# Last stage of a gated cross-attention block: row statistics of ten batches moved from VectorE to ScalarE and GpSimd

## The reference

```python
def _layernorm(x, axis=-1, eps=1e-05):
    m = jnp.mean(x, axis=axis, keepdims=True)
    v = jnp.var(x, axis=axis, keepdims=True)
    return (x - m) / jnp.sqrt(v + eps)

x = x + jnp.tanh(g_xattn[0]) * _L0_xattn_ref(_layernorm(x), ctx, ctx)
x = x + jnp.tanh(g_ffn[0]) * _L0_ffn_ref(_layernorm(x), w_gate, w_up, w_down)
x = x + jnp.tanh(g_xattn[1]) * _L1_xattn_ref(_layernorm(x), ctx, ctx, 16)
# last block: block_quant has blocks of 32 along the columns
h = einsum('bsk,nk->bsn', block_quant(_layernorm(x)), block_quant(w_fc)) + b_fc
h = jax.nn.gelu(h, approximate=False)
y = einsum('bsk,nk->bsn', block_quant(h), block_quant(w_proj)) + b_proj
x = x + jnp.tanh(g_ffn[1]) * y
```

## Time and profile before

| | |
|---|---|
| Times of three runs | 814.9, 815.8, 817.67 us; median 815.8 |
| The profiled execution | 816.15 us, of which the traced span is 814.0 us |
| Busy over the span | PE 701.7 us (86%), DVE 691.9 (85%), ACT 486.2 (60%), POOL 431.4 (53%) |
| Costliest groups of the last stage | `f_hup` on POOL 58.2 us, `f_ht` on ACT 32.4, `f_h` (gelu) on ACT 34.9 |
| Granted TensorE clock, mean of the span | 0.941 of full speed |

### The profile page before, as it was taken

The page is one execution under the profiler, slowest core; times in us unless marked ns, Lnnn a source line. Parts: engine busy times, 40 slices in busy tenths (PEclk is TensorE's granted clock), DMA queues, the critical chain, the costliest instruction groups (busy, mean ns, idle before and its releaser), DMA issues.

```text
span 814.0 us, 16554 instructions
## 1 busy us (share of the span) xinstructions
PE 701.7 (86%) x5075; PEld 516.7 (63%) x5090; DVE 691.9 (85%) x1230; ACT 486.2 (60%) x955; POOL 431.4 (53%) x331
## 2 busy tenths in 40 slices
PE   1476999999999998789999999999999876877685
PEld 1365888888888876556666666666666433544454
DVE  5996888888888878779999999989898649999995
ACT  3354555455454443348887787888788674566653
POOL 3634664656656555644445555554444526665553
PEclk9588999999999999889999999999999687999998
DMA  8800000000000000010000000000001000100011
GB/s 271 252 33 0 2 1 1 0 0 0 0 0 1 1 2 0 1 53 2 3 3 1 1 1 2 1 1 1 1 1 53 2 1 0 40 26 26 27 39 52
DMA packets 17719, 18.35 MB, mean 23 GB/s; under 512 B 1670, under 2 KB 16912, under 8 KB 17680
## 3 DMA queue, kind: packets, MB, share of 16 engines
q1 hardware_dynamic: 17084, 17.66, 6.6%
q10 hardware_dynamic: 596, 0.20, 0.1%
HBM read 13.39 MB, written 4.19 MB: 22 GB/s over the span
## 4 chain that ended last, share of the span: by engine, by line
PE 56%; DVE 22%; issue 9%; ACT 6%; POOL 3%; DMA 1%; DVEq 1%; POOLq 0%; ACTq 0%
PE ps_o L547 9%; PE a_ps_t L586 7%; PE a_ps_pv L642 7%; PE a_ps_s L627 5%; PE a_ps_m L606 5%; DVE f_ps_small L1643 4%; PE ps_gu L511 4%; PE ps_gu L513 4%; PE ps_gu L512 4%; DVE f_hcode L1659 4%; PE a_ps_t L606 3%; DVE maxima L1558 2%; PE a_ps_pv L650 2%; ACT stack_t L953 1%; ACT probs L962 1%
## 5 line engine op out<-in xcount | busy, mean ns | idle before, releaser
L962 ACT ACTIVATE probs<-a_ps_s 128x512 f32<-128x512 f32 x256 | 147.8, 602 | 29.9 <-PE a_ps_s L627 25.4
L1558 DVE TENSOR_REDUCE maxima<-a_ps_m 128x2 f32<-128x512 f32 x160 | 103.0, 686 | 11.5 <-PE a_ps_m L606 11.3
L627 PE MATMUL a_ps_s<-stack_t 64*128 64x256 f32 x512 | 101.9, 314 | 3.4 <-ACT probs L962 1.8
L1192 POOL TENSOR_TENSOR stack<-roped,stack 128x512 f32<-128x512 f32 x32 | 42.7, 1335 | 109.7 <-DVE stack L1548 108.3
L547 PE MATMUL ps_o<-w2t,hqt 128*128 128x256 f32 (+1 forms) x384 | 99.1, 392 | 1.3 <-ACT hqt L880 0.7
L511 PE MATMUL ps_gu<-w1h,yth 128*128 128x352 f32 x256 | 87.5, 342 | 9.1 <-DVE h L1364 5.9
L953 ACT CAST stack_t<-a_ps_t 128x512 fp32r<-128x512 f32 x128 | 71.8, 585 | 31.5 <-PE a_ps_t L586 31.5
L642 PE MATMUL a_ps_pv<-probs,v_aug 128*32 128x256 f32 x1024 | 84.9, 404 | 2.9 <-ACT probs L962 2.9
L586 PE MATMUL a_ps_t<-idf,stack 128*128 128x128 f32 x512 | 77.2, 292 | 8.8 <-POOL stack L1192 5.1
L512 PE MATMUL ps_gu<-w1l,yth 128*128 128x352 f32 x256 | 84.1, 328 | 0.0
L513 PE MATMUL ps_gu<-w1h,ytl 128*128 128x352 f32 x256 | 83.8, 327 | 0.0
(11 more groups left out here) (181 smaller groups left out, 1680.9 us busy)
## 6 DMA issues: line engine op xcount, KB each, us to landing
xres<-in_x SPq DMA_DIRECT2D x16, 256.0 KB, 3.2
ctx<-in_ctx SPq DMA_DIRECT2D x16, 256.0 KB, 3.8
out_x<-f_y SPq DMA_DIRECT2D x16, 256.0 KB, 2.1
w1a_raw<-in_w_gate_up SPq DMA_DIRECT2D x1, 1024.0 KB, 7.3
w_raw<-in_w_fc SPq DMA_DIRECT2D x1, 1024.0 KB, 5.7
w_raw<-in_w_proj SPq DMA_DIRECT2D x1, 1024.0 KB, 4.8
w_raw<-in_w_down SPq DMA_DIRECT2D x1, 704.0 KB, 9.7
stack_t<-neg_max_t SPq DMA_DIRECT2D x32, 8.0 KB
```

Source lines behind the costliest of these rows:

```text
L627: ins = nc.tensor.matmul(a_ps_s[:, half, n, :], a_stack_t[b.par][rows, 1, pair, kc * P:(kc + 1) * P], a_stack_t[b.par][rows, 0, pair, :], ...
L962: nc.scalar.activation(a_probs[:, u % 8], a_ps_s[:, u % 2], ACT.Exp).then_inc(a_exp, 1)
L1558: nc.vector.tensor_reduce(a_maxima[:, b.par, c, 4 * quad + half:4 * quad + half + 3:2], max_bank(m), X, ALU.max).then_inc(a_v_max, 1)
```

## The change

In bodies 0 to 9 the statistics of batch b+6 leave DVE. ACT makes them at the end of its body b: two passes over each of the two tiles, each summing its own output through `accum_out`. The first pass gives -mean/16, the second, with that as bias, the mean of squared deviations. POOL adds epsilon in an instruction of its own ahead of the power. Batches 0 to 5 keep the old way. The shift is then 16 x (-mean/16) x rstd, in the same DVE instruction as before. New tiles are `f_eps`, `f_var_eps`, `f_mean` and `f_unused` (the passes' own output, not read), and `ff_norm` gets one semaphore increment ahead of its activations.

```diff
+            def ff_input_stats(b):                       # on ACT
+                done = b.shifted(-FFN_AHEAD).count(2 * C, 0)
+                act.wait_ge(f_g_rstd, b.shifted(-2).count(1, 1))
+                act.wait_ge(f_v_shift, b.shifted(-2).count(1, 1))
+                act.sem_inc(f_alone, 1)
+                for c in range(C):
+                    nc.scalar.activation(f_unused[:, b.par, c], tiles(xres, b)[:, c, :], ACT.Identity, scale=-1.0 / (16 * D),
+                                         accum_out=f_mean[:, b.par, c:c + 1]).then_inc(f_a_stats, 1)
+                for c in range(C):
+                    act.wait_ge(f_a_stats, done + c + 1)
+                    act.sem_inc(f_alone, 1)
+                    nc.scalar.activation(f_unused[:, b.par, C + c], tiles(xres, b)[:, c, :], ACT.Square, scale=1.0 / 16,
+                                         bias=f_mean[:, b.par, c:c + 1],
+                                         accum_out=f_var[:, b.par, c:c + 1]).then_inc(f_a_stats, 1)
...
                 ff_hidden_out(b, 1)                      # ACT ff_body
+                if b.shifted(FFN_AHEAD):
+                    ff_input_stats(b.shifted(FFN_AHEAD))
...
             def ff_input_rstd(b):                        # on POOL
-                pool.wait_ge(f_v_ln, upto(V_LN1, b, "var"))
+                var = f_var[:, b.par]
+                if b.shifted(-FFN_AHEAD):
+                    pool.wait_ge(f_a_stats, b.shifted(-FFN_AHEAD).count(2 * C, 2 * C))
+                    nc.gpsimd.tensor_tensor(f_var_eps[:, :], var, f_eps[:, :], ALU.add).then_inc(f_g_var, 1)
+                    pool.wait_ge(f_g_var, b.shifted(-FFN_AHEAD).count(1, 1))
+                    var = f_var_eps[:, :]
+                else:
+                    pool.wait_ge(f_v_ln, upto(V_LN1, b, "var"))
                 if b.shifted(-2):
                     pool.wait_ge(f_a_norm, b.shifted(-2).count(C, C))
-                nc.gpsimd.tensor_tensor(f_rstd[:, b.par], f_var[:, b.par], neg_half[:, :], ALU.pow).then_inc(f_g_rstd, 1)
+                nc.gpsimd.tensor_tensor(f_rstd[:, b.par], var, neg_half[:, :], ALU.pow).then_inc(f_g_rstd, 1)
...
                                                          # DVE ff_input_shift
-                nc.vector.scalar_tensor_tensor(f_shift[:, b.par], f_mv[:, b.par, :, 0], -1.0, f_rstd[:, b.par],
+                mean, unit = (f_mean[:, b.par], 16.0) if b.shifted(-FFN_AHEAD) else (f_mv[:, b.par, :, 0], -1.0)
+                nc.vector.scalar_tensor_tensor(f_shift[:, b.par], mean, unit, f_rstd[:, b.par],
                                                ALU.mult, ALU.mult).then_inc(f_v_shift, 1)
...
                     ff_hidden_magic(b.shifted(1))        # DVE ff_body
-                if b.shifted(6):
-                    ff_input_stats(b.shifted(6))
```

More of the change, by code:

```diff
@@ L100, in build @@
         neg_half = sb("neg_half", [P, C], F32)
+        f_eps = sb("f_eps", [P, C], F32)
         loaded = [keep.enter_context(nc.semaphore(name)) for name in ("even_rows_loaded", "odd_rows_loaded")]
@@ L116, in build @@
         build_main(nc, load, loaded, out_v, g_xattn, g_ffn, w_gate_up, w_down, w_fc, b_fc, w_proj, b_proj, ident, decay,
-                   rope_cos, rope_sin, alibi, xres, ctx, gates, idf, idb, neg_half,
+                   rope_cos, rope_sin, alibi, xres, ctx, gates, idf, idb, neg_half, f_eps,
                    w1h, w1l, w2t, dec, w_fc_t, w_proj_t, bias3, ones3, tiles, weights.close)
@@ L266, in build_main @@
         f_hmag = high("f_hmag", [P, 2, F_NBH], F32)
+        f_var_eps = high("f_var_eps", [P, C], F32)
+        f_mean = high("f_neg_mean_16th", [P, 2, C], F32)
+        f_unused = high("f_unused", [P, 2, 2 * C, D], BF16)
         keep.enter_context(lasting)
@@ L356, in build_main @@
         f_alone = sem("f_waits_alone")
+        f_a_stats, f_g_var = sem("f_a_stats"), sem("f_g_var")
         def f_blocks(t):
@@ L1030, in ff_hidden_out @@
                 nc.scalar.copy(f_ht[:, b.par, c].rearrange("p k t -> p (k t)"), f_ps_h[c][:, :].bitcast(BF16)).then_inc(f_a_h, 1)
+            def ff_input_stats(b):
[8 more added lines that the diff above has]
+                    act.wait_ge(f_a_stats, done + c + 1)
+                    act.sem_inc(f_alone, 1)
+                    nc.scalar.activation(f_unused[:, b.par, C + c], tiles(xres, b)[:, c, :], ACT.Square, scale=1.0 / 16,
+                                         bias=f_mean[:, b.par, c:c + 1],
+                                         accum_out=f_var[:, b.par, c:c + 1]).then_inc(f_a_stats, 1)
             def ff_body(b):
@@ L1249, in ff_body @@
                     ff_input_rstd(b.shifted(6))
+            nc.gpsimd.memset(f_eps[:, :], EPS)
             nc.gpsimd.memset(neg_half[:, :], -0.5).then_inc(g_laid, 1)
```

## The result

The changed kernel takes 867.38 us (median of four runs, 866.08 to 869.47) against 815.35 us, a ratio of 1.063 (95% interval 1.061 to 1.065). The forecast was 875.5 with a range of 861 to 895. The profiled execution has 867.74 us, 51.6 more than the one before (816.15).

A forecast was written before the change was run, and what follows sets the result against it. DVE set the pace at 9.04 us a body; the change would close a ring of 14.86 us, ten times round: 816.15 + 58.2 + 1.5 = 875.9, less 0.35 for the median, 875.5 us, range 861 to 895.

The forecast's parts named there:

- The mechanism: Bodies 0 to 9: POOL waits for the end of ACT's body, ACT's next gelu for `f_hup`, so nothing overlaps; chance 0.87.
- The rivals: Three other outcomes: faster at 812 us (chance 0.04), table loads at 888 to 901 (0.08), no difference (0.01).
- table load: Squares beside gelu on ACT need two more loads of 1.283 us a body: 13 to 26 us more; chance 0.08.
- The rival that was faster: Statistics fit ACT's idle 3.05 us before the next gelu, POOL isn't held up: 812 us; chance 0.04.
- DVE's busy share in the stretch: Sign between `f_hup` of body 0 and of body 10: the share falls from 94% to about 54%.
- a ring of 14.86 us: Forecast time per body once round ACT's body, its statistics, POOL's small steps, `f_xup` and `f_hup`, against 9.04 before.
- signal to POOL: ACT's signal to POOL after the passes: 0.15 us taken, from 0.04 to 0.16.
- addition: POOL's epsilon addition ahead of `f_rstd`: 0.28 us until the power starts, upper end 0.67.
- loop crossings, in all: POOL's loop going round, no longer hidden in idle time: 0.3 us in each of five crossings, 1.5 us.
- the first term: End of `f_hup` to end of ACT's second `f_ht`: 6.3 us, ends 6.06 and 6.94.
- the second term: Four ACT activations over 128x256 with a sum, at the end of its body: 2.8 us, from 2.0 to 3.2.
- VectorE's relief: Taking the statistics off DVE alone, read from body 10: 0.39 us a body, 3.9 us in all.

The follow-up runs named there:

- the first experiment: Changed kernel with ScalarE's statistics passes moved from the end of its body to the start, `f_var_eps` in two halves: 812.36 us against 816.74 for the kernel before.
- The last experiment: Changed kernel with twelve idle matmuls a body on TensorE, from body 1 on, where it waits: 861.96 us, against 867.96 for the changed kernel beside it.

## Why the prediction was right

**The mechanism** was the one forecast, step by step: POOL's `f_rstd` waits for ACT's passes, `f_xup` follows it at once, the gelus wait 5.8 us for `f_hup`, `f_shift` waits on DVE, and the end of the stage is unchanged. The rivals fell as argued. No table load appears beside the squares: the changed kernel has four of 1.28 us in the whole span, as the one before, and the only one of the last stage is at the gelu's line (L1030). The rival that was faster needed the passes in ACT's idle time; the first experiment put them there, and got the 812 us that it was given. One sign came out otherwise: DVE's busy share in the stretch was to be about 54% and is 63%. 8 us of its 89 are the growth of `f_shift`, which the forecast had at nothing; without them and in a ring of 14.86 us the share would be 54%.

**The sizes.** Of the terms, with the changed kernel's body 3 beside them:

| Term | forecast | measured |
|---|---|---|
| `f_hup` to last `f_ht` | 6.3 (6.06 to 6.94) | 6.67 |
| four passes with sums | 2.8 (2.0 to 3.2) | 1.79 |
| signal to POOL | 0.15 | 0.08 |
| addition | 0.28 | 0.35 |
| `f_rstd` | 0.68 | 0.68 |
| `f_xup`, `f_hup` | 4.65 | 4.65 |
| sum | 14.86 | 14.22 |
| loop crossings, in all | 1.5 | none to be seen |

Ten times 0.65 and the 1.5 us of the crossings are the 8 us by which the forecast was too long. Part of this closeness is luck: the first term was too short by 0.37 us and the second too long by 1.01, which cancel in part. The step that was mis-sized is the second term, which came out below its lower end. I had priced a pass with sum from `f_xn`, 0.49 us start to start, and added up to 0.205 for the sum. But `f_xn` has two pointer operands. The first passes have none, take 0.40 to 0.42 us, and follow each other in 0.41; the squares have one and take 0.49 to 0.50. (That the pointer operands make the difference is not shown: the squares are another function, and `f_xn` writes float32 where the passes write bfloat16.) The read of the accumulator is an instruction of its own, 0.19 us, but it begins 0.1 us before the activation ends, and the next one starts 0.1 us before the read ends. So where an activation of 0.60 us without a sum is followed by the next after 0.49, a pass of 0.41 to 0.42 us is followed by the next after 0.41: the read adds about 0.1 us to the distance and not 0.2.

The first term was too short by 0.37 us. A falling clock was among the signs to look for, but the value was set near the best body. The last experiment shows the size: 6.67 us with the slow transposes, 6.12 with the fast ones.

The crossings of the loop cost POOL nothing visible: all ten distances between the ends of `f_hup` are 14.12 to 14.24 us, whether or not the loop goes round between them.

That **VectorE's relief** is worth little was read from body 10 and held: 0.39 us a body forecast and measured. What wasn't foreseen is that the change itself adds such a stall, since the mean now comes from SBUF: `f_shift` grew from 0.15 to 1.0 us. It lengthened nothing here: `f_xcode`, behind it on DVE, still starts before `f_hup` ends.

The best version that came out is the passes at the start of ScalarE's body with the mean through PSUM, 810.2 us, 0.8% below the kernel before. Whether its second part gains anything over the first experiment stays open: the medians differ by 2.7 us, but the intervals of their ratios overlap and the bodies are 8.65 us in both; the profiled executions differ by 2.3 us, all of it ahead of and behind those bodies.

## What to carry to other kernels

Work handed to an engine that has idle time costs nothing or a great deal, depending on where in that engine's order it stands: look up who waits for its result, what is queued behind that wait, and whether the work's own engine waits for that in turn. If so, the whole path round is the new period, and its sum can be worked out from the trace before. Here three positions of the same four passes gave 812, 835 and 867 us.

## What the hardware showed

- In the changed kernel two VectorE instructions with two SBUF operands that started under a GpSimd one ended only with it or after it, the small one no less than the large one: `f_shift` (128x2) took 0.89 to 1.00 us under `f_xup`, and 0.15 to 0.16 in the run with one operand in PSUM; `f_xcode` (128x512) took 1.46 us in body 3 and ended 0.55 us after `f_hup`, and 0.69 in the kernel before, where `f_hup` had ended. Where VectorE had started first, GpSimd's instruction was the longer one (`f_xup` 1.42 for 1.05 us beside `f_xcode`; `f_rstd` 1.49 for 0.71 beside `f_hcode`). It isn't exclusion throughout: in the kernel with the mean through PSUM `f_rstd` ran until 713.30 us, and the second `f_hcode`, begun at 712.7, still took 1.21.
- A sum through `accum_out` on ScalarE came with an instruction of 0.19 us, which overlapped its neighbours by 0.1 us at each end and so lengthened the distance between two passes by an estimated 0.1 us; the Identity passes over 128x256, without a pointer operand, followed each other in 0.41 us, the Square passes, with one, in 0.49.
- TensorE, busy for 60% of a ring of 14.2 us, ran at a mean granted clock of 0.74; with idle matmuls in that ring at 0.85, and the kernel took 861.96 us and not 867.96.
